# A post-norm decoder layer stack on one core: the first six and the last five loop iterations each get one issue order of their own, over all their samples

## What is computed

```
x = layernorm(x + self_attention(x))            # 16 heads, q = k = x, values x @ W_h
x = layernorm(x + cross_attention(x, context))  # 16 heads of 8, window of 64
for l in (0, 1):                                # two local layers
    x = x + local_attention(shift(x)) @ wo      # 8 heads of 64, l2-normed, rotary, window of 64
    x = x + (a * gelu(g)) @ w2 + b2             # a, g = split(layernorm(shift(x)) @ w1 + b1)
x = layernorm(x)
```

## Time and profile before

| what | value |
|---|---|
| time, median of 3 runs | 1413.63 us (1413.45 to 1414.42) |
| span of the profiled execution | 1410.1 us; 3.5 us less than that median |
| PE busy | 1314.7 us, 93% of the span |
| DVE, ACT, POOL busy | 1053.0, 982.9, 756.9 us |
| one round of the loop | 40.84 us |

### The profile page before, as it was taken

The page is one execution under the profiler, slowest core; times in us unless marked ns, Lnnn a source line. Parts: engine busy times, 40 slices in busy tenths (PEclk is TensorE's granted clock), DMA queues, the critical chain, the costliest instruction groups (busy, mean ns, idle before and its releaser), DMA issues. The chain is left out here.

```text
span 1410.1 us, 39538 instructions
## 1 busy us (share of the span) xinstructions
PE 1314.7 (93%) x12472; PEld 915.3 (65%) x12472; DVE 1053.0 (75%) x3190; ACT 982.9 (70%) x2694; POOL 756.9 (54%) x843
## 2 busy tenths in 40 slices
PE   6789999999999999999999999999999999998964
PEld 3456666667666667666666776666666766666653
DVE  2567887777888878778787877878787788878542
ACT  2357777777777777777777777777777777776553
POOL 1036565655656565555565655655565565655442
PEclk9899999999999999999999999999999999999785
DMA  5000000000000000000000000000000000000000
GB/s 164 11 6 4 5 8 6 6 6 4 5 2 6 6 6 6 4 6 2 6 6 6 6 4 6 4 4 6 6 6 6 4 4 4 6 5 3 3 3 4
DMA packets 22220, 12.55 MB, mean 9 GB/s; under 512 B 5879, under 2 KB 21025, under 8 KB 22177
## 3 DMA queue, kind: packets, MB, share of 16 engines
q1 hardware_dynamic: 21600, 10.96, 2.7%
q10 hardware_dynamic: 576, 1.05, 0.2%
HBM read 9.91 MB, written 2.10 MB: 9 GB/s over the span
## 5 line engine op out<-in xcount | busy, mean ns | idle before, releaser
L1192 POOL TENSOR_TENSOR local_rn<-local_sc,half_neg 128x8 f32<-128x8 f32 x128 | 211.2, 1650 | 162.4 <-DVE local_sc L1040 162.4
L855 ACT ACTIVATE local_e<-local_ps,local_bias,local_rn 128x128 f32<-128x128 f32 x512 | 233.0, 490 | 22.1 <-DVE local_bias L1053 22.1
L1213 POOL TENSOR_TENSOR local_e<-local_e,local_rd 128x512 f32<-128x512 f32 x128 | 133.3, 1041 | 130.5 <-DVE local_rd L1057 130.5
L589 PE MATMUL self_ps<-self_z,self_e 128*128 128x129 f32 x1024 | 149.9, 288 | 3.1 <-ACT self_e L782 2.1
L609 PE MATMUL local_ps<-wz,self_kT 128*128 128x512 f32 x256 | 143.1, 641 | 1.8 <-ACT self_kT L788 1.0
L974 DVE SCALAR_TENSOR_TENSOR self_y<-self_ps,self_rd,self_y 128x128 f32<-128x128 f32 x448 | 132.7, 343 | 8.1
L589 PEld LDWEIGHTS self_ps<-self_z,self_e 128*128 128x128 f32 x1024 | 130.3, 194 | 11.9 <-issue 3.0
L855 ACT ACTIVATION_READ_ACCUMULATOR local_e<-local_ps,local_bias,local_rn 128x1 f32 x512 | 121.5, 237 | 0.0
L935 DVE TENSOR_REDUCE cross_neg<-cross_ps 128x4 bf16<-128x512 f32 x128 | 82.5, 686 | 38.9 <-PE cross_ps L502 38.9
L1048 DVE TENSOR_REDUCE local_m<-local_ps 128x4 f32<-128x512 f32 x128 | 87.1, 680 | 32.6 <-PE local_ps L512 32.6
L835 ACT ACTIVATE local_sq<-local_ps 128x512 f32<-128x512 f32 x128 | 76.4, 597 | 46.1 <-PE local_ps L668 45.2
(11 more groups left out here) (172 smaller groups left out, 3383.5 us busy)
## 6 DMA issues: line engine op xcount, KB each, us to landing
self_xin<-x SPq DMA_DIRECT2D x32, 64.0 KB, 1.8
cross_cin<-ctx_in SPq DMA_DIRECT2D x32, 64.0 KB, 1.7
out<-local_out SPq DMA_DIRECT2D x32, 64.0 KB, 1.6
wqkv_s<-wqkv SPq DMA_DIRECT2D x2, 768.0 KB
wz<-w_heads ACTq DMA_DIRECT2D x4, 256.0 KB, 5.8
w_r<-w SPq DMA_DIRECT2D x2, 341.0 KB
con<-consts SPq DMA_DIRECT2D x1, 640.0 KB, 6.4
wo_s<-wo SPq DMA_DIRECT2D x2, 256.0 KB
```

The costliest lines, as they stand in the source:

```text
L589: last = nc.tensor.matmul(bank[:, 129 * j:129 * j + 129], s.e[:, h0 + j, :], s.z[:, h0 + j, :], start=True, stop=True)
L855: nc.scalar.activation(s.e[:, a, p, :], bank[:, 128 * p:128 * p + 128], ACT.Exp, bias=s.bias[:, a, p:p + 1], scale=s.rq[:, a, p:p + 1], ac ...
L1192: nc.gpsimd.tensor_tensor(s.rn[:, heads], s.sc[:, heads], half_neg[:, 0:LH], ALU.pow).then_inc(done, STEP)
L1213: nc.gpsimd.tensor_tensor(s.e[:, a, :, :], s.e[:, a, :, :], s.rd[:, a, :].unsqueeze(2).to_broadcast([128, LH // 2, 128]), ALU.mult)\
```

## The change

Each order string becomes three: one for iterations 0 to 5, the old one for the loop, and one for iterations 32 to 36. The first and the last are one weave over all their samples: a letter takes the next step of that part, and when a sample's part is finished it goes on with the next sample's. So a sample's part may start before the iteration in front of it has finished. The strings of the loop stay.

```
 ORDER_TENSOR = (
-    "ONOAAONABSPPBABPZCSZBSACAZSDSCZSCBBSCSECSDDSSDCSDEEMCCECME")
+    ("SSZZSZSSZSSSSSSSSCCZSZCSZSCSZCSCSSCSSCCSCLSAASACACSZZSZASASCDCSCZCDSSCSDSDSSDCMCCMOOAOASBACBABSZBZSCZSAASCDZSC"
...
+    ("ONOAAONABSPPBABPZCSZBSACAZSDSCZSCBBSCSECSDDSSDCSDEEMCCECME"),
...
-        def loop(eng, iteration, prepare_local, before):
...
+        def run(eng, first_iterations, iteration, last_iterations):
+
+            first_iterations()
+            if B > HELD + FILL:
+                cycle(eng, STEP * FILL, STEP * (B - HELD), iteration)
+            last_iterations()
...
+            def in_turn(letter, samples):
+
+                for n in samples:
+                    yield from placed(letter, STEP * n)
...
+            def together(order, first, last, before_local=None):
+
+                parts = tables(order)
+                if before_local is not None:
+                    parts["L"] = before_local()
+                for letter in letters:
+                    samples = [n - SKEW[letter] for n in range(first, last) if 0 <= n - SKEW[letter] < B]
+                    parts[letter] = in_turn(letter, samples)
+                weave(order, parts)
...
             def self_stage(v):
...
                 if again(v):
                     pe.wait_ge(s.acc, v)
+                    pe.wait_ge(s.z_psum, v)
...
             def mlp_head(l, v):
                 s = LOC[l]
                 pe.wait_ge(s.mid_done, v + STEP)
+                if again(v):
+                    pe.wait_ge(s.resid, v)
```

More of the change, by code:

```diff
@@ L17 @@
+import itertools
 from contextlib import ExitStack
@@ L123, in behind, with cycle @@
     return not isinstance(v, int) or v > back
+def cycle(eng, first, last, iteration):
+    with eng.Fori(first, last, STEP) as i:
+        iteration(i)
 def weave(order, parts):
@@ L352, in decoder_kernel @@
         block = ctx.enter_context(nc.Block())
-        def loop(eng, iteration, prepare_local, before):
-            fill = LAST + 1
-            for n in range(fill):
-                if n == before:
-                    prepare_local()
-                iteration(STEP * n)
-            if B > fill:
-                with eng.Fori(STEP * fill, STEP * B, STEP) as i:
-                    iteration(i)
-            for n in range(max(B, fill), B + LAST):
-                iteration(STEP * n)
+        def run(eng, first_iterations, iteration, last_iterations):
[3 more added lines that the diff above has]
+            last_iterations()
         def at(i, skew):
@@ L470, in _, with load_x, load_context @@
-            loop(nc.sync, iteration, prepare_local, 2)
+            def load_x(v):
+                if again(v):
+                    sp.wait_ge(SELF.x_copied, v)
+                sp.dma_start(SELF.xin[:, :], sample_rows(x_rows, v)).then_inc(SELF.x_loaded, 16)
+                if not again(v):
+                    sp.dma_start(con[:, 0:C_FIRST], consts[:, 0:C_FIRST]).then_inc(first_loaded, 16)
+                    prepare()
+                yield
+            def load_context(v):
+                if again(v):
+                    sp.wait_ge(CROSS.cT_psum, v)
+                sp.dma_start(CROSS.cin[:, :], sample_rows(ctx_rows, v)).then_inc(CROSS.c_loaded, 16)
+                yield
@@ new lines, in store @@
+            def store(v):
+                sp.wait_ge(LOC[1].normed, v + STEP)
+                sp.dma_start(sample_rows(out_rows, v), LOC[1].out[:, :]).then_inc(stored, 16)
+                yield
+            def iteration(i):
+                parts = {}
+                if at(i, 0) is not None:
+                    parts["S"] = load_x(at(i, 0))
+                if at(i, 1) is not None:
+                    parts["C"] = load_context(at(i, 1))
+                if at(i, SKEW["P"]) is not None:
+                    parts["P"] = store(at(i, SKEW["P"]))
+                weave(ORDER_SYNC, parts)
@@ L471, in _, with first_iterations, last_iterations @@
+            def first_iterations():
+                for n in range(FILL):
+                    if n == 2:
+                        prepare_local()
+                    iteration(STEP * n)
+            def last_iterations():
+                for n in range(B - HELD, B + LAST):
+                    iteration(STEP * n)
+            run(nc.sync, first_iterations, iteration, last_iterations)
             sp.wait_ge(stored, STEP * B)
@@ L602, in self_values @@
                         pe.wait_ge(wz_loaded[g], 16)
+                    if isinstance(v, int) and v >= Z_LAG[0]:
+                        pe.wait_ge(prep_v, PREP_V_BIAS)
                     if behind(v, Z_LAG[l] - STEP):
@@ L889, in exp_table @@
             def exp_table():
[L890 removed]
+                nc.scalar.activation(warm[:, 2:3], warm[:, 0:1], ACT.Exp)
                 yield
[L893 removed]
+            stages(nc.scalar, ORDER_SCALAR, self_stage, cross_stage, attention_head, attention_tail, mlp_head, mlp_tail,
                    self_values=self_values, gelu_table=gelu_table, exp_table=exp_table)
```

118 lines of the change are left out of this document (62 added, 56 removed).

## The result

The changed kernel takes 1402.14 us, the median of four runs (1397.25 to 1405.13), beside 1413.77 us for the kernel before on the same chip. The ratio is 0.9916, with a 95% interval of 0.9895 to 0.9937: 0.84% or 11.6 us less, where 8.3 us less were forecast (1405.3 us). The profiled execution took 1404.44 us, with a span of 1402.7 us, so what lies around the span is 1.7 us. The two profiled spans differ by 7.4 us and not by 11.6: the span of the change lies 0.6 us above its median, and that of before 3.7 us under its own.

What follows compares the result with a forecast made beforehand. The prediction took the loop to be bound by TensorE, busy 97% of it, with gains only in fill and drain. Its terms, -2.8 + 0.4 - 1.2 - 2.5 - 2.2 = -8.3 us, gave 1405.3 us, range 1394 to 1411 us.

Steps and rivals of the forecast that it cites:

- Fill, -2.8: First iterations: samples 0 and 2 start their next parts earlier, 2.8 us gained, bounds 0 and 9.6.
- the wait for the biases: Fill, before sample 0's local layers: TensorE's 2.58 us wait for VectorE shrinks, so local layer 0 starts 1.8 us earlier.
- where VectorE has room: Fill: scaled weights and tables, 1.77 us on VectorE, move some 15 us earlier, among the maxima of cross attention.
- the rival with the falling clock: Fill: a new gap drops TensorE to half clock, costing 8.8 us; slower if it lasts over 25 us, chance 0.08.
- The table of Exp, nothing: First weave: Exp's table load moves right before sample 3's exponentials; costs nothing when covered, 1.3 us if not.
- The loop, +0.4: Loop: one more register instruction and two more semaphores on TensorE per round, 0.4 us in all, 0.75 at most.
- Iteration 33, -1.2: Drain: only half of sample 29's transposes stands ahead of sample 31's cross attention output, 1.2 us less.
- my rival with the half-speed stretch: Iteration 33: the denser order closes the gap and removes the half-clock stretch, up to 8.8 us more gained, chance 0.22.
- Iteration 34, -2.5: Drain: GpSimd does sample 31's k_hat and inverse norm of q before sample 30's steps, so the bias comes 2.5 us earlier.
- The last stretch, nothing: End of the drain: sample 31's lone chain keeps its order and stays 40.2 us.
- The small moves, -2.2: Three middle stretches of fill and drain: many smaller moves win a tenth of 21.6 us idling, 2.2 us.

Runs made afterwards that it cites:

- the second measurement: The changed kernel run once more, unchanged: 1404.56 us, ratio 0.9934 against the kernel before.
- fill-only kernel: Against the changed kernel, the last five iterations go back to one after the other in the loop's string; only the first six keep new strings: 1413.13 us, ratio 1.0014.
- the two experiments: The two added TensorE waits taken out of the changed kernel's loop, 1401.06 us; both added to the kernel before, 1416.30 us.
- the kernel without loop waits: The changed kernel without its two added TensorE waits in the loop's 26 rounds: 1401.06 us, ratio 0.9921.
- the three edits together: The changed kernel without the loop's two added waits, with VectorE's tables step later in the fill and 29 unread products in the last stretch: 1389.16 us, ratio 0.9828.
- the gap was filled: The kernel with new fill and old drain plus ten unread TensorE products in iteration 33's idle times: 1410.94 us, ratio 0.9986.
- undone, 37.7 us: The changed kernel with GpSimd's new order undone in iteration 34 alone: 1409.67 us, ratio 0.9975.
- with TensorE's old string: The kernel with new fill and old drain, with GpSimd's new order put into iteration 34 alone: 1413.54 us, ratio 1.0006.
- the kernel with the last stretch filled: The changed kernel plus 29 unread TensorE products in the idle times of the last stretch: 1399.41 us, ratio 0.9897.

## Why the prediction was right, and where it was not

The sign, the range and the size hold: -11.6 us (or -9.3 by the second measurement, from its ratio) where -8.3 was forecast. But the terms behind it were off in both directions, so that the sum comes so near is in part luck.

**Fill, -2.8.** In the profiles the sum comes out near it: the loop's first store comes at 220.0 us in the mean of the nine profiles with the new fill as it is (218.3 to 223.0), and at 223.2 in the three with the old (221.0 to 224.6), 3.2 us earlier. The time of the fill-only kernel doesn't show it: -1 us, uncertain by 3. Its steps don't hold. The forecast had sample 0's L739 at 62.6 us and sample 2's self attention at 65.5; they came at 64.73 and 67.50. The wait for the biases did shrink, as forecast. What failed is that local layer 0 of sample 0 starts earlier by what this wait loses: I took cross attention ahead of it as unmoved, and its output came 2.1 us later, behind ten microseconds at half clock. That the weights and tables stand "where VectorE has room" was true of the first profile of the change; in the second and in six others they waited for their own transfer, ahead of a maximum that TensorE needs, and TensorE idled up to 4.4 us. Adding up, over windows of 1 us, TensorE's idle time and its busy time times the missing share of the clock, from 33 us to the first store: 17.8 and 4.1 us before, 10.6 and 9.1 after. The order took 7 us of idling away, and the clock took back 5 of them. That is the rival with the falling clock, at a little over half its price (8.8 us). Why the clock fell there stays open.

**The table of Exp, nothing.** Right: the load lies ahead of the exponentials, and TensorE idles 0.20 us for them, behind. From the time line of ScalarE after:

```profile
114.70 1.28 ACT L855 ACT_TABLE_LOAD   x1
116.00 1.08 ACT L855 ACTIVATE self_e<-self_ps 128x512 f32<-128x512 f32 x2
```

The exponential starts 0.02 us behind the load, so here too no drain is seen.

**The loop, +0.4.** Mis-sized: +2.0 us in the profile, and 2 to 3 by the two experiments. I priced the waits by the length of a register move on another queue, 29 ns, or 0.75 us at most in all; a round grew by 80 to 120 ns for the two.

**Iteration 33, -1.2.** The first stage gave 2.9 us. TensorE's idle time in it is 6.6 us before and 6.7 after, so all of it is work and clock, not waiting. The busy time times the missing share of the clock is 9.5 us before and 7.9 after, so 1.6 us are clock (the half-speed stretch is 17.0 us long for 20.5), and 1.3 us, counted at full clock, are work that has left the stage. The step that I forecast is there: one half of sample 29's transposes (L780, 1318.33 us) stands ahead of cross attention's output (L709, 1319.22 us), the other behind it (1321.10 us). What the whole stretch is worth the kernel without loop waits shows, whose profile had none in it:

```profile
1242.69:1318.53 75.84, 68.78 (x697) 48.70 (x698) 57.67 (x169) 56.88 (x158) 45.90 (x50) 1.00 0.02 4
```

It holds the same number of products as the change's (x697), idles 7.1 us, and is 6.6 us shorter. Of the eight profiles with this drain three (the two of the change and the three edits together) had the long stretch, two a short one (78.7 and 78.8 us) and three none (75.8 to 75.9). The old drain had it in all five (83.6 to 85.3 us), half as long where the gap was filled. So my rival with the half-speed stretch comes true in some executions with this order. These are different kernels with this stage in common; both profiles of the change itself had the long stretch, so whether its own timed executions differ by it isn't shown. Nor is it the only source of scatter: the fill-only kernel, with the old drain, goes from 1410.05 to 1419.16 us. The step that was wrong is that I took the stretch as given and counted only what stands ahead in it.

**Iteration 34, -2.5.** Mis-sized: the second stage gave 5.0 us. Counted from sample 31's input, the scores came 0.9 us earlier than before and the first bias started 1.5 us earlier and ended 2.3 us earlier, where 1.2, 2.0 and 2.7 were forecast. The rows, against the earlier trace rows:

```profile
1334.81 1.04 POOL L1276 TENSOR_TENSOR local_cosp<-local_cosp,local_rn 128x512 f32<-128x512 f32 x1
1337.05 3.26 POOL L1264 TENSOR_TENSOR local_rn<-local_sc,half_neg 128x8 f32<-128x8 f32 x2
1337.40 1.16 PE L773 MATMUL local_ps<-local_kT,local_qT 64*128 64x128 f32 x16
1339.79 0.16 DVE L1128 TENSOR_TENSOR local_bias<-local_m,local_rn 128x4 f32<-128x4 f32 x1
```

The bias no longer waits for GpSimd, as forecast. The 5.0 us are made up of 3.8 us less idle time of TensorE (11.5 to 7.7) and 3.3 us less of half clock (5.0 to 1.7 us, reckoned as in the fill), less 2.1 us of work that has come into the stage. Of the idle time the move of iteration 34 is worth 2.4 us (undone, 37.7 us), the size I gave it. But it isn't a term of its own, as I had it: with TensorE's old string it wins nothing. And the clock had no term in my sum for this stage.

**The last stretch, nothing.** Right to 0.1 us in both profiles of the change. **The small moves, -2.2**, can't be told apart from the rest.

## What to carry to other kernels

An order of instructions is a thing of all engines together: the same move on one engine was worth 2.4 us of a stage with the others' new strings, and won nothing with their old ones, so judge such a move with the strings it belongs to. Where a stage idles in part, count TensorE's clock as a term with its own rival. When one sample is left at the end, unread products in its idle time can be worth more than the order of what is left: here 5.8 us of a 40 us stretch. And count a wait added on the engine that bounds a loop by measuring the round, since 0.1 us in each of 26 rounds is 2.6 us, a quarter of what this change brought.

## What the runs showed of the hardware that I had not expected

The unread products kept the clock at 1.00 through the last stretch in one profile although idle times of up to 2.27 us stayed between them; the row of the kernel with the last stretch filled:

```profile
1372.67 0.66 PE L782 MATMUL local_ps<-con,local_e 128*128 128x128 f32 x4 [2.27 <-POOL local_e L1291]
```

In the kernel with the three edits the same idle time of 2.27 us came, and the clock was at half for 3.4 us from 1375.5 us on. In the kernel before, one idle time of 1.49 us, with shorter ones beside it, stood ahead of the half-speed stretch of 20 us:

```profile
1301.24 0.40 PE L521 MATMUL cross_ps<-cross_kb,cross_qmb 32*128 32x128 bf16 x8 [1.49 <-DVE cross_neg L935]
```

So the length of an idle time alone doesn't tell. Nor does the order: of the eight profiles with the new first stage of the drain three had the long stretch, two a short one and three none. And two waits added on TensorE made a round of 40.84 us 0.08 to 0.12 us longer.
